# Spreading the steps between batches over the sixteen heads, and giving five of them to GpSimd

## The reference, cut to what matters

```python
def _L1_xattn_ref(x, cond, mask, wq, bq, wk, bk, wv, bv, wo, bo):
    q = _w8a8_linear(x, wq, bq).reshape(B, N, H, D).transpose(0, 2, 1, 3)
    k = (cond @ wk.T + bk)...            # v alike
    scores = jnp.einsum('bhnd,bhld->bhnl', q, k) * inv_sqrt_d + mask[:, None]
    attn = jax.nn.softmax(scores, axis=-1)
    o = jnp.einsum('bhnl,bhld->bhnd', attn, v)
    return _w8a8_linear(o, wo, bo)       # rows rounded to -127..127 by their own maximum
x = x + _L1_xattn_ref(_layernorm(x, axis=-1), ctx_2048, mask_BxSxS2_ff0, ...)
```

## Time and profile before

| what | us |
|---|---|
| median of 3 runs | 796.9 |
| fastest of 3 | 796.42 |
| profiled execution | 795.17 |
| its span | 793.3 |
| head stage, first mask to the last sum into `XR` | 337.98 to 570.41 |

### The profile page before, as it was taken

How to read it: one execution, slowest core, us unless ns; L and a number is a source line. 1 busy time by engine, 2 the same in 40 slices (tenths; PEclk the granted TensorE clock), 3 DMA queues, 4 the chain that set the end, 5 groups by cost and what they waited for, 6 DMA issues and landing times. The chain is left out here.

```text
span 793.3 us, 10929 instructions
## 1 busy us (share of the span) xinstructions
PE 542.9 (68%) x3388; PEld 386.3 (49%) x3388; DVE 391.7 (49%) x1002; ACT 298.2 (38%) x631; POOL 126.2 (16%) x171
## 2 busy tenths in 40 slices
PE   0063299999999991258777687688418129999992
PEld 0043277777777770235555455465218115555550
DVE  5546666577566755354665655766342103222320
ACT  4157234433443332235645646557201003222220
POOL 1001122132213300010001101100100531222221
PEclk9995599999999995555856857868655559999996
DMA  8959100000000003001201202221240343554544
GB/s 341 404 195 343 62 11 0 10 10 10 10 0 10 1 0 127 25 1 38 81 31 52 81 35 57 70 67 59 89 135 1 90 122 62 89 92 81 84 61 114
DMA packets 22914, 62.58 MB, mean 79 GB/s; under 512 B 3778, under 2 KB 9698, under 8 KB 20826
## 3 DMA queue, kind: packets, MB, share of 16 engines
q1 hardware_dynamic: 18462, 53.47, 20.1%
q0 software_dynamic: 4416, 8.63, 6.8%
HBM read 46.40 MB, written 17.32 MB: 80 GB/s over the span
## 5 line engine op out<-in xcount | busy, mean ns | idle before, releaser
L1145 DVE CUSTOM_DVE_ANT_0 sN<-ps,maskS 100x361 f32<-100x361 f32 x128 | 65.4, 533 | 53.1 <-PE ps L755 25.1
L567 ACT ACTIVATE pE<-sN,nmx 100x361 f32<-100x361 f32 x128 | 77.4, 604 | 16.5 <-DVE nmx L1145 16.4
L763 PE MATMUL ps<-ident,pE 100*121 100x100 f32 x384 | 82.5, 353 | 1.4 <-ACT pT L558 1.2
L763 PEld LDWEIGHTS ps<-ident,pE 100*121 100x121 f32 x384 | 66.4, 248 | 33.8 <-issue 31.8
L755 PE MATMUL ps<-CT,qn 32*100 32x361 f32 x256 | 39.7, 698 | 55.3 <-DVE nmx L1145 53.1
L558 ACT COPY pT<-ps 121x300 f32<-121x300 f32 x128 | 51.6, 403 | 38.4 <-PE ps L763 37.5
L882 PE MATMUL ps<-VS,hTe 118*128 x120 | 56.7, 609 | 5.5 <-ACT hTe L605 5.5
L868 PE MATMUL ps<-CT,xT 128*128 x160 | 53.2, 477 | 2.0 <-DVE xT L1238 2.0
L1252 DVE TENSOR_TENSOR hb<-ps,b1B 128x352 f32<-128x352 f32 x20 | 10.5, 525 | 88.0 <-PE ps L868 88.0
L468 POOL DMA_INDIRECT sums_out<-yb,backI x20 | 31.0, 1550 | 109.2 <-ACT yb L615 105.3
L868 PEld LDWEIGHTS ps<-CT,xT 128*128 128x128 f32 x160 | 31.3, 197 | 24.9 <-issue 12.8
(11 more groups left out here) (233 smaller groups left out, 1118.8 us busy)
## 6 DMA issues: line engine op xcount, KB each, us to landing
VS<-in_w SPq DMA_DIRECT2D x8, 1024.0 KB, 9.2
CT<-in_ctxT SPq DMA_DIRECT2D x8, 728.0 KB, 16.9
VS<-in_ew SPq DMA_DIRECT2D x8, 708.0 KB
CT<-in_ew SPq DMA_DIRECT2D x8, 704.0 KB
slots_in<-zeros SPq DMA_DIRECT2D x5, 1056.0 KB, 12.9
xin<-slots_in SPq DMA_DIRECT2D x20, 264.0 KB, 3.4
XR<-in_x SPq DMA_DIRECT2D x1, 1600.0 KB
summB<-summary_rows SPq DMA_DIRECT2D x8, 200.0 KB
```

The lines of the kernel that those rows point to most:

```text
L567: act.activation(pE[0:S, q, 0:T], sN[0:S, q, 0:T], ACT.Exp, scale=-1.0, bias=nmx[0:S, h_:h_ + 1], accum_out=sums[0:S, j, h_:h_ + 1]).then_ ...
L763: mm = pe.transpose(ps[0:TC, 4 + r, c * S:(c + 1) * S], pE[0:S, h_ % HPC, c * TC:(c + 1) * TC], ident[0:S, 0:S])
L1145: dve.tensor_tensor_reduce(out=sN[0:S, q, 0:T], in0=ps[0:S, q, 0:T], in1=maskS[0:S, j, 0:T], scale=-1.0, scalar=3.4e38, op0=ALU.add, op1=A ...
```

## The change

On GpSimd run now, beside the inverse square root and `x + bo`: the normalised rows (`norm_x`), the query's scale and bias (`scale_q`), the value bias (`add_bv`) and the sum into `XR` (`x_out`). VectorE's steps stand at other heads (preparation at 0, 4, 5, 12, finish at 7, 9, 10, 15), and so do TensorE's and ScalarE's. The turned rows of the next batch get a buffer of their own, `xq2T`, in place of `oQT`.

```diff
-        xq2T = oQT
+        xq2T = sb(bb, "xq2T", [P, KC, S], BF16)
@@ GpSimd
+            def norm_x(b):
+                alone(g, ("rsB", b + 1), ("xq2b", b))
+                g.tensor_scalar(g2[0:S], XR[0:S, b, :], mvb[0:S, 0:1], tb[0:S, 1:2], ALU.subtract, ALU.mult)\
+                 .then_inc(sem("normed"), 1)
+            def scale_q(b, j):
+                g.wait_ge(sem("q_taken"), b + 1)
+                g.tensor_tensor(t1[:], t1[:], swqB[:], ALU.mult).then_inc(sem("q_scaled"), 1)
+                g.wait_ge(sem("q_scaled"), b + 1)
+                g.tensor_tensor(qn[:, j], t1[:], bqB[:], ALU.add).then_inc(sem("q_ready"), 1)
+            def add_bv(b):
+                g.wait_ge(sem("o_norm"), after(b + 1))
+                g.tensor_tensor(oN[0:S], oN[0:S], bvB[0:S], ALU.add).then_inc(sem("o_biased"), 1)
+            def x_out(b):
+                g.wait_ge(sem("y2"), b + 1)
+                g.wait_ge(sem("xbo"), b + 1)
+                g.tensor_tensor(XR[0:S, b, :], y2[0:S], xbo[0:S], ALU.add).then_inc(sem("x3"), 1)
             def body(b, j, u, first, last):
+                if not last:
+                    rstd_b(b + 1)
+                    norm_x(b + 1)
                 if not first:
                     with_bo(b - 1)
+                    add_bv(b - 1)
                 if not last:
-                    rstd_b(b + 1)
+                    scale_q(b + 1, 1 - j)
+                if not first:
+                    x_out(b - 1)
@@ ScalarE
-                    if h_ == 1 and not last:
+                    if h_ == 6 and not last:
                         turned_x(b + 1)
-                    if h_ == 3 and not first:
+                    if h_ == 2 and not first:
                         rows_out(b - 1)
@@ TensorE
             def rows_back(b):
                 pe.wait_ge(sem("oT_out"), after(b + 1))
-                if b < B - 2:
-                    pe.wait_ge(sem("q_ready"), b + 3)
                 pe.wait_ge(sem("x3"), after(b))
-                    if h_ == 0 and b < B - 1:
+                    if h_ == 2 and b:
+                        rows_back(b - 1)
+                    if h_ == 5 and b < B - 1:
                         pe.wait_ge(sem("xq2b"), b + 2)
-                        pe.wait_ge(sem("x3"), after(b - 1))
+                        pe.wait_ge(sem("o_norm"), after(b))
                         turn_rows(xq2b, "xq2_t", b + 1)
-                    if h_ == 2 and b < B - 1:
+                    if h_ == 7 and b < B - 1:
                         queries(b + 1)
-                    if h_ == 4 and b:
-                        rows_back(b - 1)
-                    if h_ == 9 and b:
+                    if h_ == 10 and b:
                         pe.wait_ge(sem("oQb"), after(b))
+                        if b < B - 1:
+                            pe.wait_ge(sem("q_taken"), b + 2)
                         turn_rows(oQb, "oq_t", b - 1)
@@ VectorE (prep_norm, prep_bias, finish2 and the last sum of finish5 are gone)
             def prep_scale(b, j):
+                dve.wait_ge(sem("normed"), b + 1)
             def finish3(b, j):
+                dve.wait_ge(sem("o_biased"), b + 1)
             def finish5(b, j):
                 dve.wait_ge(sem("wo_mm"), b + 1)
+                dve.wait_ge(sem("x3"), after(b))
-            finish_at = {9: finish1, 10: finish2, 11: finish3, 12: finish4, 15: finish5}
-            prep_at = {0: prep_stats, 1: prep_norm, 2: prep_scale, 3: prep_round, 6: prep_rescale, 7: prep_bias}
+            finish_at = {7: finish1, 9: finish3, 10: finish4, 15: finish5}
+            prep_at = {0: prep_stats, 4: prep_scale, 5: prep_round, 12: prep_rescale}
```

More of the change, by code:

```diff
@@ L423, in with_bo @@
                 g.tensor_tensor(xbo[0:S], XR[0:S, b, :], boB[0:S], ALU.add).then_inc(sem("xbo"), 1)
+            def add_bv(b):
[5 more added lines that the diff above has]
+                g.tensor_tensor(XR[0:S, b, :], y2[0:S], xbo[0:S], ALU.add).then_inc(sem("x3"), 1)
             def body(b, j, u, first, last):
+                if not last:
+                    rstd_b(b + 1)
+                    norm_x(b + 1)
                 if not first:
                     with_bo(b - 1)
+                    add_bv(b - 1)
                 if not last:
-                    rstd_b(b + 1)
+                    scale_q(b + 1, 1 - j)
+                if not first:
+                    x_out(b - 1)
             rstd_b(0)
+            norm_x(0)
+            scale_q(0, 0)
             g.wait_ge(sem("bvo_in"), 48)
-            batches(g, body)
+            for b in range(B):
+                body(b, b % 2, b // 2, b == 0, b == B - 1)
             with_bo(B - 1)
-            g.wait_ge(sem("xbo"), B)
+            add_bv(B - 1)
+            x_out(B - 1)
+            g.wait_ge(sem("x3"), after(B))
             g.tensor_copy(cols[:, 20:21], cols[:, 1:2]).then_inc(sem("b_done"), 1)
@@ L1074, in _ @@
             dve.wait_ge(sem("bvo_in"), 48)
-            chp, chf = chain(dve, "dve_prep", 9), chain(dve, "dve_finish", 7)
+            chp, chf = chain(dve, "dve_prep", 6), chain(dve, "dve_finish", 5)
             def row_scale(ch, rows, am, scale, inv_):
@@ L1087, in prep_stats @@
                 dve.bn_aggr(mvb[0:S], st6b[0:S]).then_inc(sem("mvB"), 1)
-            def prep_norm(b, j):
-                dve.wait_ge(sem("rsB"), b + 1)
-                chp(dve.tensor_scalar(g2[0:S], XR[0:S, b, :], mvb[0:S, 0:1], tb[0:S, 1:2], ALU.subtract, ALU.mult))
             def prep_scale(b, j):
+                dve.wait_ge(sem("normed"), b + 1)
                 row_scale(chp, g2[0:S], tb[0:S, 3:4], tb[0:S, 4:5], tb[0:S, 5:6])
@@ L1102, in prep_rescale @@
                 chp(dve.tensor_copy(sxB[:], ps[:, 7, KC * S:(KC + 1) * S]))
[L1103 to L1109, removed]
+                dve.tensor_tensor(t1[:], ps[:, 7, 0:KC * S].rearrange("p (k s) -> p k s", k=KC),
+                                  sxB[:].unsqueeze(1).to_broadcast([P, KC, S]), ALU.mult).then_inc(sem("q_taken"), 1)
             def finish1(b, j):
@@ L1118, in finish1 @@
                                   rinv[0:S].unsqueeze(2).to_broadcast([S, HEADS, HD]), ALU.mult).then_inc(sem("o_norm"), 1)
-            def finish2(b, j):
-                dve.wait_ge(sem("o_norm"), after(b + 1))
-                chf(dve.tensor_tensor(oN[0:S], oN[0:S], bvB[0:S], ALU.add))
             def finish3(b, j):
+                dve.wait_ge(sem("o_biased"), b + 1)
                 row_scale(chf, oN[0:S], tb[0:S, 6:7], tb[0:S, 7:8], tb[0:S, 8:9])
@@ L1132, in finish5 @@
                 dve.wait_ge(sem("wo_mm"), b + 1)
-                chf(dve.scalar_tensor_tensor(out=y2[0:S], in0=ps[0:S, 7, :], scalar=tb[0:S, 7:8], in1=swoB[0:S],
-                                             op0=ALU.mult, op1=ALU.mult))
+                dve.wait_ge(sem("x3"), after(b))
+                (dve.scalar_tensor_tensor(out=y2[0:S], in0=ps[0:S, 7, :], scalar=tb[0:S, 7:8], in1=swoB[0:S],
+                                          op0=ALU.mult, op1=ALU.mult).then_inc(sem("y2"), 1))
                 chf.end()
-                dve.wait_ge(sem("xbo"), b + 1)
-                dve.tensor_tensor(XR[0:S, b, :], y2[0:S], xbo[0:S], ALU.add).then_inc(sem("x3"), 1)
             def body(b, j, u, first, last):
```

## The result

The changed kernel takes 774.6 us (median of 4; 769.9 to 778.7) against 796.8: a ratio of 0.972, 95% interval 0.965 to 0.980, faster. Its profiled execution took 778.72 us, the slowest of the four, with a span of 776.6, so the two profiles differ by only 16.7 us. Ratios leave out disturbed executions, which is why a ratio and a median don't always agree.

The account below looks back on a forecast made before the run. Waits bound the kernel: a ring of 28.5 to 28.7 us per batch, partly the slow weights' DMA. Gains of 18.1, 3.8 and 1.0 less 1.3 and 1.5 make 20.1 us: 775.1 profiled, 777 median, range 768 to 787.

Parts of the forecast that it names:

- The ring: Batches 1 to 6: first mask pass to second-weights issue falls from 10.6 to 7.6 us; issue to next pass stays 18.0.
- The computation behind the issue: From second-weights issue to next first pass: computation takes 14.1 us, 16.9 at its longest, below the DMA's 18.0.
- the rival came true in one batch each: DMA's slack used up, so computation sets the period, about 27 us: 784 us; chance 0.20 together with the norm delaying passes.
- Removed idle time in group 0: Batches 1 to 6: fourth mask pass starts at 2.42 instead of 5.09 us; with an earlier turn, 3.01 gained per period.
- the array stays warm: TensorE's clock stays at its upper level, 1.3 to 1.9 us more in 6 periods: 766 to 769 us; chance 0.12.
- Batch 0: Period from batch 0 to 1, which has no DMA wait: 3.8 us gained, bounds 2 and 5.1.
- GpSimd's norm: Beside mask passes 3 and 4 of group 0: takes 0.65 us, at most 1.27, covered before head 4's reader.
- the rival that it delays passes 3 and 4: GpSimd's norm delays these group 0 passes by 0.65 us: 781 us; chance 0.20 together with the DMA's slack used up.
- The stretched step: VectorE's one-input pass took 1.48 us beside GpSimd's sum, 0.55 elsewhere; the rounding now comes after GpSimd; one hit costs 0.93.
- The last batch: Batch 7 and its end: earlier finish gains about 1.0 us; value bias and output sum on GpSimd cost 1.5, part perhaps absorbed.
- The slower rival: Next batch's first scores wait for GpSimd's two query passes, at 4 us each: about 803 us; chance 0.03.
- It doesn't do what it says: Another wait holds the fourth pass or the mix, leaving only 0.8 us per period: 790 us; chance 0.05.

Follow-up runs that it names:

- Experiment 1: Mask's DMA issued ahead of the expert's second weights: in the changed kernel 758.3 us (0.951), in the kernel before 785.0 us (0.987).
- experiment 2: Changed kernel with each expert's second weights loaded by two DMAs, 112 and 6 partitions, mask still behind them: 760.4 us, 0.948.
- experiment 1a: Changed kernel with the mask's DMA issued ahead of the expert's second weights: 758.3 us, 0.951.
- 7b: Changed kernel with, in the last batch only, the finish at its old heads 9, 11, 12 and 15: 774.5 us, 0.975.
- experiment 5: Changed kernel with 16 unread 128 x 128 products added on TensorE at the end of batches 1 to 6: 775.3 us, 0.969.
- experiment 3b: GpSimd runs its steps, but all steps stand at the heads of the kernel before: 803.3 us, 1.010.
- 3a: Steps at the heads of the changed kernel, but all on VectorE: 772.8 us, 0.971.
- experiment 4: Steps at the changed kernel's heads, all on VectorE, with the mask's DMA ahead of the second weights: 771.2 us, 0.965.
- experiment 6: Changed kernel with the mask's DMA ahead of the weights, and the first preparation and last finish back on VectorE: 754.3 us, 0.949.

## Why the prediction was right, and where its terms were off

The forecast was 777 (768 to 787); it is 774.6. Its mechanism held, but that the number came so near is partly luck. For the profiled execution the sum was 20.1 us, and the trace has 16.7: the periods gave 2.4 us more than forecast, and batch 0, the start and the last batch together 7.7 less, of which stage c gave 2.5 back; 0.6 lie in the rest. That execution was the slowest of the four; the median is 4 us lower, and no trace shows which term made the difference. Term by term:

- *The ring.* First pass to issue 7.26 us in the mean (forecast 7.6), issue to next first pass 18.13 (18.0), a middle period 25.4 (25.7), a wait for the mask's DMA at the starts. Experiment 1 shows that it was the mask's place behind the load, experiment 2 that it was the load's slowness, which set the second stretch: taking away either ends the waits, and gives 16 and 14 us by the medians. In one point the text was too sure: the waits are 1.9 to 5.0 us, up to one more than foreseen, and batch 4's start shows 0.21 us of "issue" instead.
- *The computation behind the issue* was put at 14.1 to 16.9 us. Less the waits for the mask, the second stretches leave 12.9 to 18.0 us for it, and in experiment 1a, where nothing waits for the mask, they are 14.3 to 18.0. So the slack under the DMA's 18 us was nearly used up in some batches. In the executions of 7b and of experiment 5 the rival came true in one batch each (second stretches of 20.0 and 20.1 us).
- *The rule on the spread of a load.* The Trainium skill's DMA: Bandwidth & Descriptors, "Why a DMA increments its semaphore by 16 and not by 1", makes 2 engines of 118 rows and 16 of 112. The share of 0.13 agrees with 2 of 16, and 0.75 with far more than 2.
- *Removed idle time in group 0.* 2.42 us of passes, as worked out. The 3.01 per period were 3.42 in the mean (20.5 in six against 18.1). Part of the difference is one batch that ran warm, batch 4: 5.67 us to the issue and a period of 23.8 at a clock of 0.86. So the rival "the array stays warm" came true in one batch of six, with the sign that the prediction had named against itself: in that batch's group 0 the clock was 1.00. Elsewhere its argument against the rival held, as the gap ahead of group 1's scores stayed at 4.14 us in batch 3. In the moves alone and with the mask first the rival came true widely, and there it takes the first stretch from some 7.5 to 5.7 us.
- *Batch 0.* 3.2 for 3.8, inside its bounds of 2 and 5.1.
- *GpSimd's norm* was mis-sized: 2.10 us, above the upper bound of 1.27. I took the price of a pass with constants for one with two values per partition; it also writes another type, so which difference costs the time isn't shown. The cover that I named held: VectorE waited 0.24 us at head 4 in batch 4, and the rival that it delays passes 3 and 4 didn't come. At the start GpSimd's steps cost more than the 1.3 us of the sum: the first pass came 2.6 us later, and its wait for the scores grew from 1.75 to 3.97. And in experiment 3b, where there is no cover, VectorE stands for the norm inside group 0. The sums (1.26 and 1.03 us) were as forecast.
- *The stretched step.* A mask pass at 447.53 took 0.54 us beside the norm, and a reduction at 448.31 its usual 0.69 beside the sum: no stretch, as in the sum.
- *The last batch* was the worst term: -6.3 us, where the sum had -0.5 (1.0 gained, 1.5 lost to GpSimd's steps). Of it 5.1 lie between first pass and `rows_back`, 27.4 us at a clock of 0.56 against 22.3 at 0.85, for the same 204 matmuls; 1.2 lie behind it. TensorE came to it out of the longest wait for the mask, 5.0 us. That the wait cooled it is what the windows suggest, and with products in the wait the same stretch was 24.7 us at 0.79 (experiment 5). But in 7b it was 22.8 us at 0.85 after a wait of 4.1, without products, so no experiment ties the loss to the wait. Some 2.5 us were given back, as stage c waits for a broadcast anyway; the prediction had said "part" without a number.
- *The slower rival* (`q_ready` late) is refuted: GpSimd's two passes took 2.1 us, not 6.7. But the prediction's "in time by 0.5 to 1" left too much room: at five of the six starts TensorE's weight load stood 0.5 us for `q_ready`, as at 413.28, while the matmuls ahead of it ended at the same moment. The wait for the mask behind it hid that. "It doesn't do what it says" is refuted by the 7.26 us.

What the prediction didn't see: with the mask's DMA as the bound, the moves alone give as much as the whole change, and GpSimd's part, with what it costs at the ends, is worth nothing (3a) until the bound is gone, and then some 13 us (experiment 4).

Still open: what decides which batches run warm (the same kernel spreads over 770 to 779 us), and the late finish in the last batch. Batch 1's first stretch is a case of the first: it is 8.15 us at a clock of 0.50, with TensorE busy throughout, in several of the kernels, and 5.65 us at 1.00 in others, as in experiment 6.

## What to carry to other kernels

Where a stage repeats with waits and no full engine, measure the ring: from the event that starts it to each DMA issue, and from the issue to what waits for it. Where a transfer bounds the second stretch, as here, shortening the computation gains only ahead of the issue. One line that moves the small load ahead of the big one, or splits the big one into row counts that spread, was worth 16 and 14 us more, where the whole change was worth 22. Give work to a slower engine at places where its reader comes later in order, and not at the two ends, where nothing runs beside it.

## What I had not expected of the hardware

- A GpSimd pass that subtracts and multiplies by two values per partition takes 2.10 us for 100 x 512 elements; one with constants, which writes bf16 instead of fp32, takes 1.29 us for 100 x 1024.
- A 708 KB load of 118 rows moves at 52 GB/s; as 112 and 6 rows, in the same place, it and the mask move at 172 and 246 GB/s in the windows behind their issue.
- A batch of identical work takes 20.0 us at a granted clock of 0.99 and 23.6 us at 0.78 in one execution, and the kernels differ in which batches are warm. Products put into a wait kept it at 1.00 in three batches, but not in the batch ahead of them, and where the wait was gone they were themselves 3.76 us of delay.
